# Bias rows of a mixture-of-experts FFN: a product into PSUM before, a copy into PSUM after

## What is computed

```python
x = x + gnn(layernorm(x), adj, ...)                    # 2048x2048 adjacency times 2048x512
z = layernorm(x)
probs = softmax(z @ Wr + br); w, idx = top_k(probs, 2); w = w / w.sum()
h = einsum('nc,ech->neh', z, W1) + b1                  # 16 experts, 512 -> 512
h = gelu(layernorm(h) * g1 + be1)
y = einsum('neh,eho->neo', h, W2) + b2                 # 512 -> 512
x = x + sum over the two chosen experts of w * y
```

## Time and profile before

| what | value |
|---|---|
| time, median of 3 runs | 498.26 us (497.08 to 501.61) |
| profiled execution, its own time | 497.92 us |
| its span, first to last instruction | 496.2 us |
| PE busy | 462.0 us (93%) |
| DVE busy | 348.7 us (70%) |
| ACT busy | 286.0 us (58%) |
| POOL busy | 226.3 us (46%) |
| mean rate of all DMA | 176 GB/s |

### The profile page before, as it was taken

The page is one execution under the profiler, slowest core; times in us unless marked ns, Lnnn a source line. Parts: engine busy times, 40 slices in busy tenths (PEclk is TensorE's granted clock), DMA queues, the critical chain, the costliest instruction groups (busy, mean ns, idle before and its releaser), DMA issues.

```text
span 496.2 us, 10201 instructions
## 1 busy us (share of the span) xinstructions
PE 462.0 (93%) x2297; PEld 382.7 (77%) x2298; DVE 348.7 (70%) x735; ACT 286.0 (58%) x472; POOL 226.3 (46%) x269
## 2 busy tenths in 40 slices
PE   0699999999999999979999999999999999999990
PEld 0488888877888888867788888888788787888870
DVE  5798864777788877885666676676887676767620
ACT  1666462474544334444668667678777866787450
POOL 4355330342155637652464545544545526444532
PEclk9999999999999999998999999999999999999996
DMA  8621224893645644248857876867789778564443
GB/s 283 284 65 63 87 64 170 287 320 128 225 157 180 205 136 138 91 118 294 259 119 222 237 202 147 225 141 200 214 229 294 232 221 228 139 151 85 86 65 42
DMA packets 31387, 87.26 MB, mean 176 GB/s; under 512 B 5984, under 2 KB 6128, under 8 KB 30848
## 3 DMA queue, kind: packets, MB, share of 16 engines
q1 hardware_dynamic: 17488, 56.54, 34.0%
q0 software_dynamic: 9264, 22.02, 21.8%
q10 hardware_dynamic: 4608, 8.39, 4.6%
HBM read 67.79 MB, written 19.14 MB: 175 GB/s over the span
## 4 chain that ended last, share of the span: by engine, by line
PE 75%; DMA 11%; DVE 4%; issue 3%; ACT 2%; POOL 1%; POOLq 1%; DVEq 1%; SPq 1%; ACTq 0%
PE ps L1564 15%; PE ps L1807 11%; PE ps L1813 10%; PE ps L1810 10%; PE ps L1548 6%; PE ps L1536 6%; DMA out<-y_sb,scat_i 3%; PE ps L1668 3%; PE ps L1721 3%; PE ps L1829 3%; PE ps L1604 2%; DMA xg<-xn_rows,tok_i 2%; DMA w_raw<-in_w 2%; PE ps L1524 1%; DMA xn_rows<-xn 1%
## 5 line engine op out<-in xcount | busy, mean ns | idle before, releaser
L1009 ACT ACTIVATE g_sb<-ps,be_sb,g_sb 128x128 f32<-128x128 f32 x152 | 57.1, 456 | 49.7 <-PE ps L1829 49.7
L769 POOL DMA_INDIRECT out<-y_sb,scat_i x35 | 60.6, 1731 | 40.6 <-DMA out<-y_sb,scat_i 25.8
L1442 DVE TENSOR_TENSOR w_split<-w_raw,w_split x56 | 66.0, 1220 | 9.9 <-issue 9.0
L742 POOL DMA_INDIRECT xg<-xn_rows,tok_i x40 | 44.4, 1109 | 58.8 <-ACT gate L961 47.6
L1450 DVE TENSOR_SCALAR h_hat<-ps,h_mv,h_rs 128x512 f32<-128x512 f32 x38 | 30.7, 808 | 42.3 <-issue 27.3
L827 ACT ACTIVATE adj_hi<-adj_raw,small 128x1024 fp32r<-128x1024 f32 x32 | 36.8, 1150 | 40.6 <-PE ps L1564 34.6
L995 ACT ACTIVATE w_split<-w_raw x28 | 53.0, 1913 | 7.4 <-DMA w_raw<-in_w 4.9
L1132 DVE SCALAR_TENSOR_TENSOR adj_lo<-adj_raw,small,adj_hi 128x1024 fp32r<-128x1024 f32 x32 | 40.8, 1276 | 20.1 <-ACT adj_hi L827 20.0
L1564 PE MATMUL ps<-sup,adj_lo 128*128 128x512 f32 x192 | 49.2, 398 | 0.0
L1564 PE MATMUL ps<-sup,adj_hi 128*128 128x512 f32 x192 | 49.2, 398 | 0.0
L653 POOL TENSOR_SCALAR rstd<-mv 128x1 f32<-128x1 f32 x15 | 13.8, 918 | 66.9 <-DVE mv L1172 66.8
(11 more groups left out here) (212 smaller groups left out, 962.7 us busy)
## 6 DMA issues: line engine op xcount, KB each, us to landing
w_raw<-in_w SPq DMA_DIRECT2D x64, 512.0 KB
adj_raw<-in_adj_steps SPq DMA_DIRECT2D x32, 512.0 KB, 3.5
out<-x_sb ACTq DMA_DIRECT2D x16, 256.0 KB, 2.8
xn_rows<-xn ACTq DMA_DIRECT2D x16, 256.0 KB, 3.0
x_sb<-in_x SPq DMA_DIRECT2D x3, 1024.0 KB, 13.1
gw_raw<-in_gnn_w SPq DMA_DIRECT2D x1, 1024.0 KB, 5.6
x_sb<-in_x SPq DMA_DIRECT2D x2, 512.0 KB, 7.5
xg<-xn_rows,tok_i POOLq DMA_INDIRECT x40, 4.2
```

Of the source, the lines that this page charges most:

```text
L742: return pool.indirect_dma_start(to, None, xn_rows, bass.IndirectOffsetOnAxis(ap=tok_i[:, s:s + 1], axis=0)).then_inc(landed[s % 2], 16)
L769: pool.indirect_dma_start(out, bass.IndirectOffsetOnAxis(ap=at, axis=0), y_sb[:, par, :], None, compute_op=ALU.add).then_inc(scattered[par ...
L1009: ins = act.activation(g_sb[:, par, c * P:(c + 1) * P], ht_ps(par)[:, c * P:(c + 1) * P], ACT.Gelu, scale=g1_sb[:, bass.ds(e * C + c, 1)], ...
L1442: ins = dve.tensor_tensor(w_parts(n, 1, e + 1, 2 * h, 2), w_raw[:, n, :, :].rearrange("p a n -> p (a n)")[:, at], w_parts(n, 0, e + 1, 2 * ...
```

## The change

Both bias products and the way to their split rows go. The host repeats each bias row 128 times, so a whole 128x512 tile of float32 (256 KB) is loaded per expert and layer straight from the input, in the same place of SyncE's queue. This tile is copied into the PSUM bank before the layer's twelve products, which all accumulate: layer one's by DVE, as a third step of its slot (three slots ahead), layer two's by ACT, as the first step of its slot. Three banks that had last been written only in part get one product with the start flag beforehand (clear_h, clear_y). For the early slot ACT copies all three bias rows. The early slot uses bank 4 in place of 5, slot 0's layer one bank 5 in place of 4, and the words of the plan bank 2 in place of 3. `split_bias`, `store_biases`, the zero fills and POOL's bias loads go. In the diff the first `slot_seed` and `slot` are ACT's, the second `slot_seed` and the list under it are DVE's.

```diff
-            def load_bias(n, e, ring):
-                sp.dma_start(bias_row[n][0:2, ring].bitcast(F32), bias_dram[n, e]).then_inc(raw_in[n], 16)
+            def load_bias(n, at, ring):
+                sp.dma_start(bias_rows[n][:, ring], (b1, b2)[n][at, :]).then_inc(raw_in[n], 16)
...
+            def early_seed(dst, n, e):
+                act.wait_ge(raw_in[n], 96 - 32 * n)
+                act.activation(dst, bias_rows[n][:, e * D:(e + 1) * D], ACT.Copy).then_inc(e_seeded, 1)
...
             gate_exp(3)
+            act.wait_ge(acc_read, T - 1)
+            early_seed(e_h_ps, 0, 0)
             finish_t(T - 2)
+            act.wait_ge(acc_read, T)
+            early_seed(h_ps(0, 0), 0, 1)
...
             gate_exp(4)
+            act.wait_ge(e_h_hat_ok, 1)
+            early_seed(e_y_ps, 1, 0)
             act.preload_act_table(ACT.Gelu)
...
+            def slot_seed(s, par, e):
+                act.wait_ge(raw_in[1], e * 48 + 48)
+                act.wait_ge(y_ok, s + 1)
+                act.activation(y_ps(par), bias_rows[1][:, bass.ds((e & 3) * D, D)], ACT.Copy).then_inc(y_seeded, 1)
...
             def slot(s, par, word, landed, last=False):
+                slot_seed(s, par, e_s)
                 slot_gelu(s, par, e_s)
...
+            def slot_seed(s, par, e):
+                dve.wait_ge(raw_in[0], e * 48 + 48)
+                if not isinstance(s, int) or s > 2:
+                    dve.wait_ge(h_hat_ok, s - 1)
+                dve.tensor_copy(h_ps(s, par), bias_rows[0][:, bass.ds((e & 3) * D, D)]).then_inc(h_seeded, 1)
...
                 slot_h_hat(s + 1, 1 - par)
                 slot_g_lo(s, par)
+                slot_seed(s + 3, 1 - par, expert_in(word, par + 3))
                 split_next(1, expert_in(earlier, 1 - par), starts_in(earlier, 1 - par))
...
-            def bias_product(dst, n, row):
-                pe.matmul(dst, two_rows[:, :], bias_row[n][:, row], start=True, stop=False)
+            def clear_h():
+                pe.matmul(h_ps(1, 1), ident_r[:, :], tab_rows[:, :], start=True, stop=True).then_inc(h_cleared, 1)
+            def clear_y(par):
+                pe.matmul(y_ps(par), ident_r[:, :], tab_rows[:, :], start=True, stop=True).then_inc(y_cleared, 1)
...
                 pe.wait_ge(split_hi[n], e + 1)
-                bias_product(dst, n, bass.ds((e & 3) * D, D))
+                pe.wait_ge((h_seeded, y_seeded)[n], s + n)
                 pe.wait_ge(hi_ok, s + 1)
...
-        "b1": np.asarray(L0_ffn_b1),
+        "b1": np.repeat(np.asarray(L0_ffn_b1), P, axis=0),
```

More of the change, by code:

```diff
@@ L97 @@
 GATED = BATCHES[0:3] + ((11, 5),)
-BIAS_OUT_IN, BIAS_IN = 6, 8
+BIAS_IN = 8
 LN_EPS = 1e-5
@@ L275, in gnn_moe_program @@
         xn_t = place("xn_t", [P, 2, D], F32)
-        b_raw = place("b_raw", [P, D], F32)
+        e_g = place("e_g", [P, D], F32)
+        e_y = e_g[:, :]
         end_gnn = where[0]
-        bias_row = [place(f"bias_row{n}", [P, 4 * D], F32R) for n in (1, 2)]
+        bias_rows = [place(f"bias_rows{n}", [P, 4 * D], F32) for n in (1, 2)]
         e_xg = place("e_xg", [P, ROW], F32)
@@ L464, in gnn_moe_program, with h_ps @@
         compact_ps = ps[:, 7, 0:TAB]
[L465 to L468, removed]
+        e_x_ps, e_h_ps, e_h_t_ps, e_y_ps = ps[:, 6, :], ps[:, 4, :], ps[:, 1, :], ps[:, 4, :]
+        e_x_hi, e_x_lo = early_hi_sb, early_lo_sb
+        e_g_hi, e_g_lo = early_hi_sb, early_lo_sb
+        words_ps = ps[:, 2, 0:3 * TAB]
         def xt_ps(par):
             return ps[:, par, :]
-        def h_ps(par):
-            return ps[:, 4 - par, :]
+        def h_ps(s, par):
+            return ps[:, 5 if isinstance(s, int) and s == 0 else 4 - par, :]
         def ht_ps(par):
@@ L546, in load_static @@
                 sp.wait_ge(split_lo[n], e - 1)
[L547 to L554, removed]
+                load_layer(n, slice(e * P, (e + 1) * P), e % 2, slice(e % 4 * D, (e % 4 + 1) * D))
             def first_weights(i):
@@ L1028, in _ @@
             act.sem_inc(y_ok, 2)
+            act.wait_ge(y_cleared, 2)
+            slot_seed(0, 0, expert_in(word, 0))
             slot_gelu(0, 0, expert_in(word, 0))
@@ L1470, in _ @@
             rest = dve.value_load(pairs[0:1, 0:1], min_val=E // 2 - 2, max_val=SLOTS // 2 - 2)
+            dve.wait_ge(h_cleared, 1)
+            slot_seed(1, 1, expert_in(word, 1))
             early_lo(1, 1, 0)
@@ L1474, in _ @@
                 early_lo(1, 1, piece)
+            dve.wait_ge(e_y_ok, 1)
+            slot_seed(2, 0, expert_in(word, 2))
             slot_g_lo(0, 0)
@@ L1479, in _ @@
             slot_x_lo(3, 1)
+            slot_seed(3, 1, expert_in(word, 3))
             slot_stats(2, 0)
@@ L1482, in _ @@
             slot_g_lo(1, 1)
+            slot_seed(4, 0, expert_in(word, 4))
             split_next(0, expert_in(word, 2), starts_in(word, 2))
@@ L1673, in early_part @@
                     ins = pe.matmul(dst, act_part[:, c * P:(c + 1) * P], w_part(n, low, 0, c),
-                                    start=False, stop=last and c == C - 1)
+                                    start=False, stop=last and c == C - 1, skip_group_check=True)
                 return ins
@@ L1726, in first_part @@
                 for c in range(C):
-                    ins = pe.matmul(h_ps(0), act_part[:, 0, c * P:(c + 1) * P], w_part(0, low, 1, c),
-                                    start=False, stop=last and c == C - 1)
+                    ins = pe.matmul(h_ps(0, 0), act_part[:, 0, c * P:(c + 1) * P], w_part(0, low, 1, c),
+                                    start=False, stop=last and c == C - 1, skip_group_check=True)
                 return ins
```

80 lines of the change are left out of this document (30 added, 50 removed).

## The result

The kernel after took 501.89 us (median of 17 runs, 498.32 to 505.0), the kernel before 497.08 us beside it (17 runs). The ratio is 1.0089, with a 95% interval of 1.0068 to 1.0110: slower by 0.9%, where 502.6 us and slower by 0.9% had been forecast. The sum came out; its terms did not all do so.

The account below looks back on a forecast made before the run. PE was taken to bound the loop, DVE second by 0.45 us per slot and then in PE's place. 497.9 + 0 before the loop + 6.7 in it - 2.0 after it = 502.6 us, slower by 0.9%; range 490 to 512 us.

Parts of the forecast that it names:

- PE's part: Loop: without the bias products PE's slot falls 0.45 us to 6.36 us, 13.5 us over 30 slots if PE stayed the bound.
- The copy's price: Loop: DVE's added copy into PSUM costs 0.35 to 0.73 us per slot; 0.60 us was taken.
- DVE's list: Loop: DVE's own work of 190.8 us, 6.36 us per slot, grows to 208.8 us (201.3 to 212.7) with the copy.
- slots near 7.0 us where an expert has two: Sign of being right, in the loop: PE's slots near 7.0 us where an expert has two.
- The waits that stay: Loop: DVE keeps 1.5 us of waiting for products and 2.5 us of the 5.5 us of room for POOL.
- DMA's part: Loop: 256 KB bias loads in place of 4 KB stretch weights and scatters on the chain; 1.5 us taken.
- The bound of 6.4: Loop, 375 to 408 us: 6.4 us if weights and both scatters on the chain all stretch by a quarter.
- the prediction's own signs of being wrong: PE's slots at 6.4 us throughout, a 0.43 us copy, or ACT waiting longer for raw weights between 350 and 410 us.
- the rival that DMA becomes the bound: Chain through weights and scatters, 375 to 408 us, stretches by its whole quarter: 507.5 us; chance 0.17.
- ACT's part: Loop: one copy per slot, at most 19 us into 49.6 us of room; costs nothing unless weight splits are late.
- The end: After the loop: three slots without weight splits and two layer-two blocks save 2.0 us (0 to 2.5).
- Before the loop: Removed bias products offset by three ACT copies, a clearing product and a slower gather: zero in sum (-1.5 to +2).

Follow-up runs that it names:

- the kernel with neither copy nor loads: Kernel after without DVE's layer-one bias copies in the loop and with bias loads of 2 rows (4 KB) instead of 128: 489.99 us, ratio 0.985.
- small loads: Kernel after with every bias load 2 rows (4 KB) instead of 128 (256 KB), all copies kept: 496.86 us, ratio 0.998; repeated 496.56 us, ratio 1.000.

## Why the prediction was right, and where its steps were not

**PE's part: right for a slot, not for the loop.** Slots without a wait take 6.33 to 6.42 us; 6.36 was forecast. But in the kernel with neither copy nor loads the loop wins 3.8 of the 13.5 us.

**The copy's price: right.** 686 ns, and 0.60 us from start to start.

**DVE's list: the step that was wrong in form.** The prediction took the list as 6.36 us in every slot ("DVE is second to PE by only 0.45 us per slot") and made a mean of 208.8 us out of it. The list is uneven: 13.68 us in the pair at 284.62 us of the kernel before, and in the pair at 312.79 us, which has no split, 13.08 us of which 3.25 are waits for PE. So in 18 slots PE got its gain in spite of the copy, and in 12 copy and loads together cost more than PE had gained. The expected picture, "slots near 7.0 us where an expert has two", was right in kind and too small: pairs with two sets of splits or more take 6.6 to 8.0 us a slot, and single slots up to 9.1. Taking the copy away gave 9.5 us, where the mean list had made it cost 18.

**The waits that stay.** DVE's wait for products is 0.9 us (1.5 forecast), for POOL 7.6 us over all (2.5 forecast as what stays of 5.5, besides the 6.2 that can't go: 8.7).

**DMA's part: mis-sized.** 1.5 us was taken; the loads measured 5.0 and 5.3 us beside the copy, 2.4 at most without it. The bound of 6.4 held. One of the prediction's own signs of being wrong came: ACT was not to wait longer for raw weights between 350 and 410 us, and it waits 8.8 us there (the three places in the view above) where the kernel before had

```profile
ACT w_split L995 <- DMA w_raw<-in_w: 4.9, 2, 3.3
```

So the rival that DMA becomes the bound was right in part, beside the forecast and not in its place. The waits are partly where they were looked for. The DMA pieces among the longest of the chain of waits of the kernel after, from 245 to 425 us, which answer to the earlier trace rows:

```profile
259.50 4.83 DMA bias_rows<-in_b
351.42 7.34 DMA w_raw<-in_w
365.90 8.77 DMA w_raw<-in_w
376.32 10.15 DMA w_raw<-in_w
405.32 8.50 DMA w_raw<-in_w
420.14 6.42 DMA w_raw<-in_w
```

Before, the same stretch of the chain had one load of weights, of 9.67 us, and two scatters; now a bias load stands on it by itself at 259.50 us, where the prediction had not looked.

**ACT's part: right in the loop** (0.4 us), wrong at the end. There no other slot covers the copy. ACT's and PE's timelines at the end of the kernel after:

```profile
480.46 0.69 ACT L979 ACTIVATE y_sb<-ps,gate 128x512 f32<-128x512 f32 x1 [1.04 <-PE ps L1823]
481.66 0.60 ACT L1011 ACTIVATE ps<-bias_rows 128x512 f32 x1 [0.51 <-ACT y_sb L979]
482.20 1.49 ACT L1000 ACTIVATE g_sb<-ps,be_sb,g_sb 128x128 f32<-128x128 f32 x4
484.70 1.19 PE L1815 MATMUL ps<-w_split,gt_hi 128*128 x4 [0.78 <-ACT gt_hi L1005]
```

Without the copy the last gelu could start at 481.15 us, when its transposition (480.41 + 0.66 = 481.07) and the gating ahead of it on ACT (480.46 + 0.69) have ended; it starts at 482.20, behind the copy, and PE waits 0.78 us. The end saved 0.7 us, not 2.0.

**Before the loop** 1.4 us went, where nothing had been taken (-1.5 to +2). This is not clear of chance: the kernel before with DVE's loop written out, whose work ahead of the loop is the same, begins the last transposition ahead of the loop at 238.06 us in its profiled execution, the kernel before at 240.01 and the kernel after at 239.07.

In sum: loop +4.9 (forecast +6.7), start -1.4 (0), end -0.7 (-2.0), against each other +2.8 us of span; between the medians it is 4.8. By runs, from the kernel before: the kernel with neither copy nor loads gave 7 us, the loads then took 2.4 back and DVE's copy 9.5. These steps add up by their making, since each begins where the one before it ends, and their sizes hang on the order: beside small loads the copy costs 6.9 us (496.86 against 489.99), beside the copy the loads cost 5.0. That the forecast of 502.6 lay so close is partly luck, errors of opposite sign: PE's gain was 7 us for 15.5, the copy cost 9.5 for 18, the loads up to 5 for 1.5.

What made the 12 slots late besides the splits (the rest of PE's waits in the kernel with neither) was not taken apart further: raw weights, scatters ahead of POOL's power and DVE's splits all stand in it. In that kernel the two longest pairs of DVE's list, 15.43 us from 242.69 and 15.50 from 390.05, hold 3.5 and 4.7 us of waits for POOL's power.

## What to carry to other kernels

Where two engines are close, compare their lists slot by slot, or in the heaviest pair and the lightest one, and not by the mean: work moved to the second engine can be free in light slots and cost nearly its full time in heavy ones, and the first engine can't collect its gain there. Ask of a gap not only how long it is but what the step put into it must be ready for, and what the step itself must wait for. A larger load on a queue that feeds the critical splits can cost time though the DMA engines are not full on the average: here up to 5 us, with a busy share of 0.79 in the loop and 0.90 in its fullest part.

## What the runs showed that was not expected

PE's two longest waits cost more than themselves. Stretches of the kernel after around its longest wait (2.65 us, ending at 392.23 us), with the columns of the first view above:

```profile
388.00:391.00 3.00, 1.58 (x7) 0.96 (x6) 1.91 (x2) 2.97 (x7) 0.46 (x1) 1.00 0.89 240
391.00:394.00 3.00, 1.77 (x9) 1.77 (x10) 3.00 (x6) 3.00 (x5) 1.59 (x2) 0.62 1.05 317
394.00:397.00 3.00, 3.00 (x12) 2.47 (x12) 0.91 (x3) 2.97 (x8) 2.15 (x2) 0.81 1.04 423
397.00:400.00 3.00, 3.00 (x14) 2.41 (x14) 2.28 (x4) 2.48 (x4) 1.02 (x1) 1.00 0.82 180
```

and PE's timeline there:

```profile
388.51 1.07 PE L1823 MATMUL ps<-w_split,xt_hi 128*128 x4
392.23 1.11 PE L1839 MATMUL ps<-k_sb,h_hat 128*128 128x128 f32 x4 [2.65 <-DVE h_hat L1441]
393.85 1.75 PE L1815 MATMUL ps<-w_split,gt_hi 128*128 x4
400.00 0.60 PE L1839 MATMUL ps<-k_sb,h_hat 128*128 128x128 f32 x4
```

Behind the wait the granted clock is 0.62 and then 0.81, that is, partly at the lower of its two levels (1.2 GHz in place of 2.4). The transposition takes 1.11 us where others take 0.60, four products 1.75 where others take 1.17, and the slot 7.77 us where one without a wait takes 6.4. So 1.4 us come on top of the 2.65. The next longest wait, 2.15 us up to 441.88 us, is alike: the granted clock is 0.50 from 443 to 446 us, and the slot takes 8.02 us. Behind the waits of 1.38, 1.58 and 1.72 us that end at 293.21, 259.93 and 376.68 us the slots take 6.41. In the kernel before, whose PE hardly waits, the clock is 1.00 through the whole loop. A change that trades an engine's steady pace for a shorter one with waits can pay this too; the prediction had no term for it.
